# Attention: products by V four chunks at a time, and the copy of turned tiles at the head of each ScalarE and VectorE step

## The reference, cut to what matters

```python
qkv = (x @ Wqkv + bqkv).reshape(B, L, 3, n_heads, head_dim)
q, k, v = (qkv[:, :, 0], qkv[:, :, 1], qkv[:, :, 2])
scores = jnp.einsum('bqhd,bkhd->bhqk', q, k) / math.sqrt(head_dim)
bias = -jnp.abs(pos[None, :] - pos[:, None])
scores = scores + slopes[None, :, None, None] * bias[None, None]
probs = jax.nn.softmax(scores, axis=-1)
out = jnp.einsum('bhqk,bkhd->bqhd', probs, v).reshape(B, L, D)
...
```

## Time and profile before

| | |
|---|---|
| median of three runs | 3335.37 us |
| the profiled execution: its own time | 3327.31 us |
| its span in the profile | 3325.7 us |
| share of the span busy: TensorE, VectorE, ScalarE, GpSimd | 92%, 70%, 54%, 32% |
| first scores to last maximum of the attention stage | 355.1 to 1370.2 us |
| in it: transposes, scores, V products on TensorE | 548.9, 368.2, 273.7 us busy |
| maxima and copies on VectorE | 622.7, 262.8 us busy |
| exponentials and copies on ScalarE | 592.5, 356.8 us busy |

### The profile page before, as it was taken

The page is one execution under the profiler, slowest core; times in us unless marked ns, Lnnn a source line. Parts: engine busy times, 40 slices in busy tenths (PEclk is TensorE's granted clock), DMA queues, the critical chain, the costliest instruction groups (busy, mean ns, idle before and its releaser), DMA issues. The chain is left out here.

```text
span 3325.7 us, 57653 instructions
## 1 busy us (share of the span) xinstructions
PE 3059.6 (92%) x19234; PEld 2293.6 (69%) x19234; DVE 2327.6 (70%) x4173; ACT 1806.2 (54%) x3126; POOL 1072.7 (32%) x949
## 2 busy tenths in 40 slices
PE   6999799999999999789997899899999999768887
PEld 5777577777777777577775777688888888634443
DVE  5563688888888888645563699845555444589996
ACT  3332699999999999523222323232222222159995
POOL 3333422232232232234442356531111110016666
PEclk9999899999999999899999899999999999889999
DMA  6774422222232232446643644421111110301212
GB/s 209 240 256 177 111 78 62 77 86 65 63 95 66 63 98 65 138 171 213 229 165 130 182 140 138 145 97 45 45 43 42 43 45 23 118 7 55 67 45 76
DMA packets 239349, 350.51 MB, mean 105 GB/s; under 512 B 31792, under 2 KB 129104, under 8 KB 239184
## 3 DMA queue, kind: packets, MB, share of 16 engines
q1 hardware_dynamic: 208256, 290.41, 27.2%
q0 software_dynamic: 8912, 32.82, 3.0%
q10 hardware_dynamic: 22016, 25.17, 2.1%
HBM read 210.68 MB, written 137.64 MB: 105 GB/s over the span
## 5 line engine op out<-in xcount | busy, mean ns | idle before, releaser
L913 DVE CUSTOM_DVE_ANT_0 attend_probs<-attend_scores,attend_bias_table 128x1024 f32<-128x1024 f32 x512 | 622.7, 1217 | 110.6 <-PE attend_scores L754 100.3
L833 ACT ACTIVATE attend_probs<-attend_probs,attend_neg_max 128x1024 f32<-128x1024 f32 x512 | 592.5, 1157 | 89.1 <-DVE attend_neg_max L913 85.2
L770 PE MATMUL attend_turned<-ident,attend_probs 128*128 128x128 f32 x4096 | 548.9, 275 | 2.0 <-ACT attend_probsT L842 1.8
L770 PEld LDWEIGHTS attend_turned<-ident,attend_probs 128*128 128x128 f32 x4096 | 476.6, 140 | 90.7 <-ACT attend_probsT L842 14.9
L754 PE MATMUL attend_scores<-attend_k_stack,attend_q_stack 96*128 96x512 f32 x1024 | 368.2, 441 | 15.4 <-DMA attend_q_stack<-qk_parts 15.4
L842 ACT COPY attend_probsT<-attend_turned 128x512 f32<-128x512 f32 x640 | 356.8, 577 | 1.1 <-PE attend_turned L770 1.0
L2273 DVE TENSOR_TENSOR cross_ffn_h_lo<-cross_ffn_hidden,cross_ffn_h_hi 128x512 fp32r<-128x512 f32 x128 | 104.5, 822 | 337.3 <-ACT cross_ffn_h_hi L2164 336.6
L716 POOL TENSOR_TENSOR attend_out_parts<-attend_out_full,attend_out_parts 128x256 fp32r<-128x256 f32 x64 | 46.9, 733 | 754.5 <-ACT attend_out_parts L850 754.5
L785 PE MATMUL attend_out_acc<-attend_probsT,attend_v_in 128*32 128x256 f32 x4096 | 273.7, 385 | 0.7 <-DVE attend_out_full L933 0.7
L922 DVE COPY attend_probsT<-attend_turned 128x512 f32<-128x512 f32 x384 | 262.8, 684 | 2.2 <-PE attend_turned L770 2.1
L2161 ACT ACTIVATE cross_ffn_hidden<-cross_ffn_h_acc,cross_ffn_b_cols 128x512 f32<-128x512 f32 x128 | 88.2, 689 | 267.1 <-PE cross_ffn_h_acc L2068 243.6
(11 more groups left out here) (296 smaller groups left out, 6665.7 us busy)
## 6 DMA issues: line engine op xcount, KB each, us to landing
qk_parts<-qkv_qk_out SPq DMA_DIRECT2D x64, 512.0 KB, 3.2
attend_k_stack<-qk_parts SPq DMA_DIRECT2D x192, 128.0 KB, 2.5
attend_q_stack<-qk_parts SPq DMA_DIRECT2D x192, 128.0 KB, 2.7
qkv_wq_raw<-L_ffn_w POOLq DMA_DIRECT2D x16, 1024.0 KB, 7.8
o_parts<-attend_out_parts ACTq DMA_DIRECT2D x64, 256.0 KB, 2.5
carried_o_in<-o_parts SPq DMA_DIRECT2D x32, 512.0 KB, 6.4
qkv_x_in<-x SPq DMA_DIRECT2D x8, 1024.0 KB, 6.0
v_rows<-qkv_v_out SPq DMA_DIRECT2D x32, 256.0 KB, 3.4
```

Of the source, the lines that this page charges most:

```text
L770: last = pe.transpose(turned[:, bank, c], probs[:, i % 4, k * P:(k + 1) * P], ident[:, :])
L833: act.activation(probs[:, i % 4], probs[:, i % 4], ACT.Exp, bias=neg_max[:, i % 4:i % 4 + 1], scale=-1.0, accum_out=den[:, qg % 2, j, h:h ...
L913: dve.tensor_tensor_reduce(probs[:, i % 4], scores[:, i % 2], bias_table[:, h, at:at + T], -1.0, BIG, ALU.add, ALU.min, neg_max[:, i % 4:i ...
```

## The change

TensorE issues the V products of four chunks behind units 3 and 7 of a group, in place of two chunks behind units 1, 3, 5 and 7. ScalarE's step becomes copy(i-1), exp(i+1); VectorE's becomes copy(i-1), maximum(i+2). The number of instructions, their shapes and all waits are the same.

```diff
@@ -802,8 +802,8 @@  (TensorE, before)
                     if exists(turn, qg, 1):
-                        if k % 2 == 1:
-                            for c in range(k - 1, k + 1):
+                        if k % 4 == 3:
+                            for c in range(k - 3, k + 1):
                                 times_v(turn, qg, c)
@@ -873,13 +873,13 @@  (ScalarE, body)
                     for i in range(UNITS):
-                        if not (final(turn) and i + 1 >= UNITS):
-                            exp(*shifted(turn, i, 1))
                         if not (isinstance(turn, int) and turn == 0 and i == 0):
                             t, k = shifted(turn, i, -1)
                             copy(t, k, 0)
                             if k % 4 == 3:
                                 copy(t, k, 1)
+                        if not (final(turn) and i + 1 >= UNITS):
+                            exp(*shifted(turn, i, 1))
                         before(turn, i)
@@ -943,12 +943,12 @@  (VectorE, body)
                     for i in range(UNITS):
-                        if not (final(turn) and i + 2 >= UNITS):
-                            maximum(*shifted(turn, i, 2))
                         if not (isinstance(turn, int) and turn == 0 and i == 0):
                             t, k = shifted(turn, i, -1)
                             if k % 4 != 3:
                                 copy(t, k)
+                        if not (final(turn) and i + 2 >= UNITS):
+                            maximum(*shifted(turn, i, 2))
                         before(turn, i)
```

## The result

| | before | after |
|---|---|---|
| median of the runs | 3335.5 us (4 runs) | 3491.7 us (4 runs, 3485.3 to 3493.7) |
| ratio to before, 95% interval | | 1.0472 [1.0457, 1.0487] |
| the profiled execution | 3327.3 us | 3493.7 us |
| its span | 3325.7 us | 3492.1 us |
| one group | 15.92 us | 18.30 us |

The forecast was 3475 us, from 3435 to 3525. The change costs 156 us by the medians, 140 were forecast.

A forecast was written before the change was run, and what follows sets the result against it. TensorE was taken to bound the kernel at 15.92 us a group; a ring of waits through VectorE's copy would make it 18.14. 63 x 2.22 = +139.9 us on 3327.3 gives 3467, plus 8 for the median: 3475 us, range 3435 to 3525.

The forecast's parts named there:

- What bounds before: Attention stage: TensorE sets the pace, its steps sum to 15.68 of 15.92 us a group, 0.24 us left for waits.
- Part 1: TensorE's V products in fours: block 1.88 us, boundary 0.31; two boundaries fewer, -0.62 us a group if TensorE stays bound.
- Part 2: ScalarE copies before it exponentiates: removes the transposes' wait, at most 0.24 us a group; alone a gain of 0 to 15 us.
- Part 3, the ring: VectorE copies before its maximum: transposes, copy, maximum, scores wait in a circle; group 18.14 us, +2.22; chance 0.87.
- T: Time in us within a stretch between V block ends, 0 at the first scores; the stretch was laid out to 8.66.
- restarting a waiting TensorE: Part of the range: each restart of TensorE after a wait may cost a few hundredths, up to +10 us.
- The other queues: SyncE's reloads of V and GpSimd's bias tables: both costed at nothing, with several microseconds of cover.
- The sum: Whole kernel: 63 groups x 2.22 = +139.9 us, 3467 us for the profiled execution, 3475 us for the median.
- the 0.62 us of reciprocal and widening: VectorE's two instructions in the stretch behind unit 7, between maximum(i+4) and the next copy, counted in full at 0.62 us.
- the clock: Rival: TensorE's clock falls as it idles; a tenth of its work at 1.2 GHz adds 95 us, 3570 us; chance 0.06.
- TensorE stays the bound: Rival: VectorE keeps up, a group takes 15.06 us, -54 us, 3281 us; chance 0.05.

The follow-up runs named there:

- S: ScalarE's copy put ahead of its exponential, as the only change to the kernel before: 3311.0 us, ratio 0.9944.
- V: VectorE's copy put ahead of its maximum, as the only change to the kernel before: 3492.3 us, ratio 1.0480.
- B: V products in blocks of four chunks, as the only change to the kernel before: 3402.5 us, ratio 1.0216.
- the run with opposed orders and GpSimd's wait: Kernel before with blocks of four and VectorE's copy first, ScalarE's exponential still first, GpSimd held until VectorE's widening copy is done: 3569.1 us, ratio 1.0709.

## Why the prediction was right, point by point

- **What bounds before.** The steps of TensorE sum to 15.68 us and the rest is waits for ScalarE's copy. Right: S alone removes these, and its groups take 15.64 us.
- **Part 1, 1.88 us for a block and 0.31 for a boundary.** Right in size: 1.86 us, and 15.37 us for three blocks. The 109 ns that the Trainium skill (TensorE: Matmul & The Clock Gate, Back-to-back issue gap) gives for a single matmul of 256 columns do not hold for a float32 round of four: four more of them lengthened a block by 0.86 us. Not foreseen in the text: with the old ScalarE order the long block costs 1.05 us a group by itself.
- **Part 2, a gain of 0 to 15 us.** A little low: alone it gained 19 us by the ratio (0.0056 x 3335). Beside V it is worth far more: 111 us with the contention with GpSimd taken out of both (3569.1 to 3458.1).
- **Part 3, the ring.** Right. Without VectorE's order the change is faster than before, work moved out of the ring comes off in full, and work put into TensorE's waits costs nothing. In the trace the chain runs as laid out. Behind unit 7 the copy starts at T = 1.65 and the maximum at 2.26 (forecast 1.64 and 2.24); behind unit 3, where no reciprocal stands in the way, scores(i+7) start at 5.25 and the stretch ends at 8.65 (5.26 and 8.66). So the up to 10 us that the range allows for restarting a waiting TensorE, for which no row stood, did not appear. That V alone costs 160 us is no test of this ring: there the ring goes through ScalarE. What V costs depends on its partners: 2.46 us a group alone, 0.93 with S, 2.58 with B, 2.62 with both.
- **The other queues.** Only half right. SyncE's loads stayed hidden. GpSimd I cost at nothing by looking at its waits; what it costs is the length of a VectorE instruction beside it.
- **The sum.** 140 us of cost forecast, 156 measured, inside the range. The term that was mis-sized is the 0.62 us of reciprocal and widening, read from a group in which GpSimd ran beside it for less long (the copy took 0.48 us there, 0.63 here and 0.29 alone): it measured 0.78, which is 10 us over 62 steps. The second is the clock, set apart as a rival with 0.06: it came as seven stretches worth 11 us, not a tenth of the time. 62 x 2.22 = 138, with 10 and 11 that is 159 us, what lies between the first and last L797. The profiled executions differ by 166 us, the medians by 156; 3.7 us lie ahead of the first L797 and 3 us behind the last. The causes of these two stay open, and so does why before ran 8 us faster when it was profiled. Against the profiled execution, from which all rows come, the forecast was 27 us short (3467 for 3493.7); that the median lies only 17 above 3475 is in part luck.
- **The rival "TensorE stays the bound".** It needed maximum(i+5) by T = 4.0. In the trace scores(i+7) start at T = 5.25 behind unit 3 and, after a wait of 0.92 us for it, at 6.06 behind unit 7. Wrong with the change's VectorE order. Without it the kernel is faster than before, but by 12 us of the 54 that this rival gave (15.68 us a group where it said 15.06).

## What to carry to other kernels

Ask of each step order what the engine in front of it is waiting for: a copy whose input comes from the bound engine may go first on one engine (ScalarE, whose copy frees a bank) and ruin the pace on another (VectorE, whose maximum frees the scores). Where engines pass work round in a ring, write out the ring once with start-to-start steps and the long block in it; such sums gave the usual group of seven variants within 0.3 us here, while busy shares said that every engine had slack. Fewer, longer blocks pay only as long as the others have work left through the block. With ScalarE's copy first, three blocks behind units 0, 3 and 6 beat both four and two; behind units 1, 4 and 7 they beat two, and their interval overlaps that of four.

## What the runs showed of the hardware that was not expected

- VectorE's widening copy (float32, from SBUF to SBUF, 128x256) takes 0.29 us alone, 0.49 before, 0.64 in the changed kernel and up to 3.5 us beside a bias table of GpSimd; each time that it is long it ends 0.15 us behind the GpSimd instruction that was running when it started. Held apart by one wait it took 293 to 295 ns in all 64 groups. The Trainium skill (SBUF — State Buffer, SBUF: two separate sides) says that VectorE in its two-port mode and GpSimd take a shared pair of ports for a whole instruction, and that the later one blocks; the trace agrees, with these numbers. That this copy ran in the two-port mode no row shows.
- In the changed kernel the granted clock fell to 1.2 GHz seven times in the stage, each time behind two waits of 0.6 and 0.9 us without a matmul, with transposes and scores between them, and it stayed at 1.00 in the same places once 11 short matmuls filled the waits. It also stayed at 1.00 in the run with opposed orders and GpSimd's wait, where TensorE was busy for 0.84 of 400 to 1360 us, against 0.88 in the changed kernel. So the busy share of the whole stage does not tell whether it falls.
